# Second attention's keys: three products into separate columns of the array, from a context laid out by kind of token

## What is computed

```python
y_dca, y_main = y[:, -DCA:, :], y[:, :-DCA, :]              # DCA = 16 of 64 tokens
kv_dca = (y_dca @ Wkv_dca + bkv_dca).reshape(b, DCA, 2, H, HD)
k_dca = _ln(kv_dca[:, :, 0], kn_dca_w, kn_dca_b)
q = _ln((x @ Wq + bq).reshape(b, s1, H, HD), qn_w, qn_b)    # H = 16 heads of HD = 16
kv = concatenate([y_main @ Wk + bk, y_main @ Wv + bv])      # split by head
k = _ln(kv[..., :HD], kn_w, kn_b)
ctx = attn(q, k, v) + attn(q, k_dca, v_dca)                 # two softmaxes, added
return ctx @ Wo + bo
```

## Time and profile before

| | us |
|---|---|
| median of 3 runs | 1023.98 |
| lowest and highest run | 1020.61, 1028.11 |
| the profiled execution's own time | 1022.1 |
| its span, first to last instruction | 1020.3 |
| of it outside the span | 1.8 |

### The profile page before, as it was taken

How to read it: one execution, slowest core, us unless ns; L and a number is a source line. 1 busy time by engine, 2 the same in 40 slices (tenths; PEclk the granted TensorE clock), 3 DMA queues, 4 the chain that set the end, 5 groups by cost and what they waited for, 6 DMA issues and landing times. The chain is left out here.

```text
span 1020.3 us, 25737 instructions
## 1 busy us (share of the span) xinstructions
PE 865.4 (85%) x9240; PEld 668.7 (66%) x9240; DVE 676.6 (66%) x1581; ACT 424.1 (42%) x1011; POOL 335.0 (33%) x293
## 2 busy tenths in 40 slices
PE   0799999999999899999889999999999770089882
PEld 0477777777777688989757777777776650056551
DVE  5577777778777675555367777777776479556660
ACT  1244434444344342233455555566555680022220
POOL 1443433434334040000033333333333010147763
PEclk9999999999999999999999999999999995589995
DMA  9300000000000000000011111111111099855542
GB/s 296 93 13 17 15 11 15 10 15 15 10 15 31 2 8 4 0 0 0 3 17 25 25 30 31 31 31 31 28 26 32 16 338 319 218 161 94 87 75 31
DMA packets 74907, 56.61 MB, mean 55 GB/s; under 512 B 40945, under 2 KB 70001, under 8 KB 74865
## 3 DMA queue, kind: packets, MB, share of 16 engines
q1 hardware_dynamic: 68720, 46.62, 16.3%
q0 software_dynamic: 6144, 9.44, 5.5%
HBM read 41.81 MB, written 14.22 MB: 55 GB/s over the span
## 5 line engine op out<-in xcount | busy, mean ns | idle before, releaser
L404 ACT ACTIVATE pr_t<-bank 128x512 f32<-128x512 f32 x128 | 76.4, 597 | 159.7 <-PE bank L300 158.9
L824 POOL TENSOR_TENSOR g_k_bd<-g_k_t,head_mask 128x1024 f32<-128x1024 f32 x32 | 60.6, 1895 | 134.8 <-ACT g_k_t L999 134.8
L312 PEld LDWEIGHTS bank<-v_bd,pr_t 128*64 128x64 f32 x2048 | 70.0, 137 | 26.5 <-issue 26.3
L300 PE MATMUL bank<-ident,sub 128*128 128x128 f32 x512 | 82.3, 283 | 3.6 <-ACT pr_t L404 2.9
L312 PE MATMUL bank<-v_bd,pr_t 128*64 128x18 f32 x2048 | 82.8, 214 | 0.1
L300 PEld LDWEIGHTS bank<-ident,sub 128*128 128x128 f32 x512 | 56.0, 141 | 30.8 <-issue 17.2
L481 DVE TENSOR_TENSOR sub<-bank,top 128x2048 f32<-128x2048 f32 x32 | 73.3, 2292 | 3.9 <-DVE top L477 0.2
L261 POOL TENSOR_TENSOR rot<-part_a,part_b 128x512 f32<-128x512 f32 x32 | 40.8, 1274 | 103.4 <-DVE part_b L490 103.4
L477 DVE TENSOR_REDUCE top<-bank 128x32 f32<-128x2048 f32 x32 | 73.1, 2285 | 0.5 <-PE bank L288 0.4
L819 POOL TENSOR_TENSOR xres<-xres,g_out_bias 128x256 f32 (+1 forms) x32 | 23.4, 731 | 150.7 <-DVE g_xn L1022 150.7
L648 ACT ACTIVATE f_hid<-bank,b 128x128 f32<-128x128 f32 x128 | 36.6, 368 | 85.5 <-PE bank L594 85.5
(11 more groups left out here) (204 smaller groups left out, 2052.0 us busy)
## 6 DMA issues: line engine op xcount, KB each, us to landing
e_w_gu<-in_experts_in SPq DMA_DIRECT2D x11, 768.0 KB, 10.7
table<-r_row SPq DMA_DIRECT2D x16, 320.0 KB, 8.5
e_w_d<-in_experts_out SPq DMA_DIRECT2D x11, 384.0 KB, 12.7
xres<-in_x SPq DMA_DIRECT2D x4, 1024.0 KB, 9.6
out<-xres SPq DMA_DIRECT2D x32, 128.0 KB, 1.7
xres<-in_experts_in SPq DMA_DIRECT2D x3, 768.0 KB, 21.0
keys_in<-in_ctx_t SPq DMA_DIRECT2D x32, 64.0 KB, 1.8
vals_in<-in_ctx_t SPq DMA_DIRECT2D x32, 64.0 KB, 1.8
```

Of the source, the lines that this page charges most:

```text
L300: m = pe.transpose(b_pr[:, j * P:(j + 1) * P], sub[:, v, cols], k.ident[:, :])
L312: m = pe.matmul(b_o[64 * b:64 * b + 64, hp * VW0:(hp + 1) * VW0], pr_t[:, e, j, b * S:(b + 1) * S], v_bd[:, v, b, hp, :], start=True, stop ...
L404: act.activation(pr_t[:, e, :, :].rearrange("p j q -> p (j q)"), b_pr[:, :], ACT.Exp).then_inc(a_exp, 1)
L824: pool.tensor_tensor(k_bd[:, v, :, :, :, :].rearrange("p c b h s -> p (c b) h s"), k_t[:, v, :, :].rearrange("p c (b a s) -> p (c b) a s", ...
```

## The change

On the host a second copy of the context, `ctx_by_kind`, is laid out: for each tile its 96 main tokens (48 of each batch), and then its 32 DCA tokens (16 of each). `g_keys_in` becomes one plane of 128 token columns, filled by one transfer, without zeros. The key product becomes three: main tokens 0 to 63 into rows 0 to 63 of PSUM, main tokens 64 to 95 into rows 64 to 95, DCA tokens into rows 96 to 127. The built program gives the first an array tile of 128 x 64 at column 0, and the two others tiles of 128 x 32 at columns 64 and 96. Each of them writes its rows alone, so nothing is added up. Key rows are now in the order of kinds; the bias table is loaded in that order, and ScalarE's write of the keys (L999) puts the columns back into the order of tokens. The values keep their two zero-filled planes.

```diff
-            sp.wait_ge(g_fill, 2)
-            def load(dst, done, used, t, i, u):
+            sp.wait_ge(g_fill, 1)
+            def both(t, i, u):
                 if later(t, 2):
-                    sp.wait_ge(done[u], 32 * i)
-                    sp.wait_ge(used, t - 1)
+                    sp.wait_ge(keys_done[u], 16 * i)
+                    sp.wait_ge(g_qkp, t - 1)
+                sp.dma_start(keys_in[:, u, :], ins["ctx_by_kind"][:, bass.ds(t * P, P)]).then_inc(keys_done[u], 16)
...
-            pool.memset(keys_in[:, :, :, :], 0.0).then_inc(g_fill, 1)
...
-                    pe.wait_ge(keys_done[u], 32 * (i + 1))
+                    pe.wait_ge(keys_done[u], 16 * (i + 1))
...
-                    for kind in range(2):
-                        m = pe.matmul(b_qk[:, D:2 * D], keys_in[:, u, kind, :], k.wcen[:, (2 + kind) * D:(3 + kind) * D],
-                                      start=(kind == 0), stop=(kind == 1))
+                    for kind, rows in ((0, slice(0, 64)), (0, slice(64, 2 * MAIN)), (1, rows_of_kind[1])):
+                        m = pe.matmul(b_qk[rows, D:2 * D], keys_in[:, u, rows], k.wcen[:, (2 + kind) * D:(3 + kind) * D],
+                                      start=True, stop=True)
                     m.then_inc(g_qkp, 1)
...
-                        act.activation(k_t[:, v, :, :].rearrange("p c (b s) -> p (c b) s", b=2)[:, :, cols],
-                                       b_qk[:, D:2 * D].rearrange("p (c s) -> p c s", s=S)[:, :, cols], ACT.Identity,
+                        act.activation(k_t[:, v, :, :].rearrange("p c (b s) -> p c b s", b=2)[:, :, :, cols],
+                                       b_qk[:, D:2 * D].rearrange("p (c m) -> p c m", m=P)[:, :, rows_of_kind[kind]]
+                                       .rearrange("p c (b s) -> p c b s", b=2), ACT.Identity,
...
-            (k.wcen[b * S + first:b * S + first + count, keys], over_rows(bias, count))
-            for b in range(2) for first, count, bias in ((0, MAIN, ins["main_k_b"]), (MAIN, DCA, ins["L1_xattn_bkv_dca"][0:D]))] + [
+            (k.wcen[0:2 * MAIN, keys], over_rows(ins["main_k_b"], 2 * MAIN)),
+            (k.wcen[2 * MAIN:P, keys], over_rows(ins["L1_xattn_bkv_dca"][0:D], 2 * DCA))] + [
```

More of the change, by code:

```diff
@@ L727, in second_attention @@
         z = Scope(nc, stack, "right")
-        keys_in = z.sb("g_keys_in", [P, 2, 2, P])
+        keys_in = z.sb("g_keys_in", [P, 2, P])
         vals_in = z.sb("g_vals_in", [P, 2, 2, P])
@@ L763, in second_attention @@
         kinds = ((0, slice(0, MAIN), MAIN), (1, slice(MAIN, S), DCA))
+        rows_of_kind = (slice(0, 2 * MAIN), slice(2 * MAIN, P))
         DEPTH = 5
         def sync(sp):
-            sp.wait_ge(g_fill, 2)
-            def load(dst, done, used, t, i, u):
+            sp.wait_ge(g_fill, 1)
+            def both(t, i, u):
                 if later(t, 2):
-                    sp.wait_ge(done[u], 32 * i)
-                    sp.wait_ge(used, t - 1)
+                    sp.wait_ge(keys_done[u], 16 * i)
+                    sp.wait_ge(g_qkp, t - 1)
+                sp.dma_start(keys_in[:, u, :], ins["ctx_by_kind"][:, bass.ds(t * P, P)]).then_inc(keys_done[u], 16)
+                if later(t, 2):
+                    sp.wait_ge(vals_done[u], 32 * i)
+                    sp.wait_ge(g_v, t - 1)
                 rows = ins["ctx_t"][:, bass.ds(t * P, P)].rearrange("c (b s) -> c b s", b=2)
                 for kind, cols, _ in kinds:
[L776 to L781, removed]
+                    sp.dma_start(vals_in[:, u, kind, :].rearrange("c (b s) -> c b s", b=2)[:, :, cols],
+                                 rows[:, :, cols]).then_inc(vals_done[u], 16)
             def store(t):
@@ L801, in gpsimd @@
             pool.memset(v_bd[:, :, :, :, :], 0.0).then_inc(g_fill, 1)
-            pool.wait_ge(g_fill, 4)
+            pool.wait_ge(g_fill, 3)
             for h in range(2):
@@ L810, in gpsimd @@
                         pool.tensor_scalar(ones, ones, k.kind[rows, kind:kind + 1], None, ALU.add).then_inc(g_fill, 1)
-                pool.wait_ge(g_fill, 4 + 4 * (h + 1))
+                pool.wait_ge(g_fill, 3 + 4 * (h + 1))
             pool.wait_ge(k.g_obias, 1)
@@ L949, in scalar @@
         def scalar(act):
-            act.wait_ge(g_fill, 4 + 8)
+            act.wait_ge(g_fill, 3 + 8)
             def square(tk, v):
@@ L1829, in lay_out @@
     laid["ctx_t"] = np.ascontiguousarray(a["ctx_1024"].reshape(T, C).T)
+    pairs = np.asarray(a["ctx_1024"]).reshape(NT, 2, S, C)
+    laid["ctx_by_kind"] = np.ascontiguousarray(np.concatenate(
+        [pairs[:, :, 0:MAIN].reshape(NT, 2 * MAIN, C), pairs[:, :, MAIN:S].reshape(NT, 2 * DCA, C)], axis=1).reshape(T, C).T)
     laid["pos_rows"] = np.ascontiguousarray(a["fside_BxSx2_0"].reshape(NT, P, 2).transpose(1, 0, 2))
```

## The result

The changed kernel takes 1033.22 us (median of 6 runs, 1031.49 to 1037.88) against 1024.57 for the kernel before (6 runs, 1020.61 to 1028.11): 8.65 us more. The ratio is 1.0096, with a 95% interval of 1.0070 to 1.0121: slower, though by less than 1%. The forecast said 8.7 us more. The interval reaches from 7.2 to 12.4 us, so the size is confirmed no better than that by the medians, and the agreement to 0.05 us is luck.

What follows compares the result with a forecast made beforehand. The prediction took the repeating cycle from the key product's end over VectorE and ScalarE to L924 as the bound. 0.28 us more in each of 31 steps made +8.7 us, 1023.98 to 1032.7 us, range 1013 to 1038.

Steps and rivals of the forecast that it cites:

- The bound: Second attention: the 8.89 us step is the cycle from L944's end, 4.0 us of VectorE and ScalarE, L924, back to L944.
- The terms: Added to L944's end: two changes of shape, 0.10 and 0.095, first loads 0.055 and 0.03, second tile under 0.01; 0.28 us.
- L942 to L944: Start of the query product to start of the key product: 1.07 us, from 0.97 and a change of shape.
- The first load of 32 columns: First weight load of the 32-wide key products: no row had one, taken as half the 64-wide load, 0.03 us.
- L863 behind the first record of L944: Next step's L863 to start 1.15 us behind the first key product record, before 0.86.
- Idle ahead of L924: TensorE's wait before the transposes of g_hat: to fall from 0.33 to 0.17 us a step.
- The choice: Key product: 32-wide products wait until the 64-wide one is through, four pitches as before; 0.28 us a step more, chance 0.58.
- The rival with tiles side by side: All three key products run together despite their shapes: L944 ends 0.26 us sooner a step, 1015.9 us; chance 0.20.
- The interleaved rival: Key passes go A, BC, A, BC with three changes of shape inside: 0.59 us a step, 1042.3; interleaved or serial, chance 0.13.
- The cover: TensorE work between L944's end and L924 has 0.30 to 0.39 us of cover, hiding L863's added 0.16.
- The rest at nothing: Key transfer, wait, dropped memset, fewer bias loads and ScalarE's reading order: hidden, taken as 0.
- The count of 31 steps that pay: Of 32 key products the first is followed by feed-forward work, so 31 pay 0.28 us each, +8.7 us.

Runs made afterwards that it cites:

- repeat_covered: Kernel before, with two transposes of L863's first group done twice, between the key product's end and L924: step 8.890 us, ratio 1.0007.
- repeat_paid: Kernel before, with two transposes of g_hat at L924 done twice: step 9.108 us, ratio 1.0058.
- hat_early: four_32 with g_hat ahead of VectorE's second maximum: ratio 0.9786; its group: same edit on the kernel before, 0.9892, and with keys ahead of the query product, 0.9811.
- four_32: Changed kernel with its 64-wide key product cut in two, so four products with tiles of 128 x 32: step 8.625 us, ratio 0.9908 to the kernel before.
- two_64: Changed kernel with keys as two 64-row products, DCA tokens' own weights left out (keys not right): step 8.620 us, ratio 0.9909 to the kernel before.
- layout_alone: Changed kernel's layout, transfers and ScalarE read, but two full key products again (keys not right): step 8.892 us, ratio 0.9983 to the kernel before.
- keys_first: Changed kernel with its three key products ahead of the query product, right behind L877: step 9.008 us, ratio 1.0056 to the kernel before.

## Why the prediction was right

*The bound.* The cycle from the end of L944 over VectorE and ScalarE to L924 was read from the earlier trace rows alone; `repeat_covered`, `repeat_paid` and the `hat_early` group show it.

*The terms.* L942 to L944: 1.07 forecast, 1.06 measured. The 64-wide passes 0.27 apart and 0.31 to the next shape: as forecast. The first load of 32 columns: taken as 0.03, measured 0.024. L863 behind the first record of L944: 1.15 forecast, 1.13 measured. The step: 9.17 forecast, 9.168 measured. Idle ahead of L924: 0.17 forecast, 0.20 measured. With 31 steps of 0.277 the sum is 8.6 us; the medians differ by 8.65, with the interval from 7.2 to 12.4 us. The step confirms the size, to about 0.01 us; the medians confirm its sign and its order of magnitude. Of the 0.277, the terms that were forecast measure 0.268 (two changes of shape at 0.093 for 0.10 and 0.095, loads of 0.051 and 0.024 for 0.055 and 0.03, the second tile 0.007), a little under the 0.28 to 0.29 that they added up to. The 0.009 behind the keys was in no term, and makes up for most of it: so far the match of the sum is luck.

*The choice.* The step on which the sign hung was that a 128 x 32 product waits for a running 128 x 64 one in other columns. No row of before showed it; it was inferred from each change of shape costing the same 0.09, one between two tiled shapes among them, and had 0.58 plus its neighbours' chance. The records above, and `four_32` and `two_64` against the changed kernel, show it. By the rule of the Trainium skill, "TensorEngine Tiling (Array Packing)", Key Properties, that a change of the tiling mode drains the engine, it had to be so; the trace agrees, and adds the price, 0.093 us. The rival with tiles side by side had nearly the right price, 0.26 us a step gained, for what one shape brings (0.267 and 0.271).

*The interleaved rival* falls with the four record lines: one change of shape inside, not three. The first passes of all tiles stand ahead of the second ones only while the shape is one.

*The cover.* Stated as 0.30 to 0.39, it was read too low by about 0.16 and a first load: the edit of `hat_early` took out 0.33 of it where the idle time showed 0.22. That erred on the safe side here and changed no term.

*The rest at nothing.* `layout_alone` confirms it as one sum, to within 0.4% of the time; how much each part of it weighs was not tried apart. The count of 31 steps that pay was not tried apart either.

Left open: what sets off the stretches at a lower clock that make single executions several us longer. They were averaged over, not explained. Nor is it known whether the one in the filling of the second attention goes with the new layout, as the twelve profiles suggest.

## What to carry to other kernels

When a product is cut into pieces for separate columns of the array, cut all of them to one tile shape: four of 32 gained 0.27 us a step where 64 + 32 + 32 lost 0.28, with one product fewer and the same data. Count changes of shape between neighbours as well, at 0.09 us and a bare weight load each, and place a tiled group beside one of its shape. Before that, find the cycle that repeats and which engine has cover where: an engine that was busy for 96% of the time took 0.22 us of added work free of charge in one part of its step and paid for it in full in another, and the largest gain, 0.33 us a step, came from the order of two instructions on another engine.

## What the runs showed of the hardware

At the full granted clock, 2.4 GHz: a change of tile shape costs 0.091 to 0.094 us beyond a pass's pitch, whether rows or columns change and whether or not the tiles overlap. The first weight load behind it is bare and goes with its columns: 0.024 us for 32, 0.051 for 64, 0.104 for 128 (0.056 in the transposes of L863 and L896). Directly behind a group of its own shape it did not show (L919 behind L863, the keys behind L877 in `keys_first`). Tiles of one shape start 0.007 us apart and share a pitch of 0.216 us for a pass of 256 columns, the four of L853 as the eight of L288.
